# Part of the probabilities-times-values product in three fp32r passes, x loaded twice, and layer norm tails by token tile

## What is computed

```
def _layernorm(x): return (x - mean(x)) / sqrt(var(x) + 1e-5)
# 1: cross-attention, 32 query heads of 128, 4 key/value heads, 4096 + 256 keys
q = latents @ Wq;  k = concat(context, latents) @ Wk;  v = concat(context, latents) @ Wv
attn = softmax(q k^T / sqrt(128));  out = (attn @ v) @ Wo
# 2: linear attention, 32 heads, scores times a causal decay
qkv = silu(h @ qkv_w.T);  scores = q k^T * decay (zero above the diagonal);  attn = scores @ v
normed = norm_w * attn * rsqrt(mean(attn * attn) + EPS)
out = (sigmoid(h @ gate_w.T) * normed) @ out_w.T
# 3: a mixture of 4 low-rank experts of rank 16, the best two weighted by a softmax
x = x + xattn(_layernorm(x), ctx);  x = x + attn(_layernorm(x));  x = x + ffn(_layernorm(x))
```

## Time and profile before

| | us |
|---|---|
| median of three runs | 2026.29 (2024.20 to 2031.31) |
| the profiled execution | 2030.37 |
| its span | 2028.5 |
| TensorE busy in the span | 1987.3 (98%) |
| VectorE, ScalarE, GpSimd busy | 1245.9, 947.0, 776.0 |

### The profile page before, as it was taken

How to read it: one execution, slowest core, us unless ns; L and a number is a source line. 1 busy time by engine, 2 the same in 40 slices (tenths; PEclk the granted TensorE clock), 3 DMA queues, 4 the chain that set the end, 5 groups by cost and what they waited for, 6 DMA issues and landing times. The chain is left out here.

```text
span 2028.5 us, 27101 instructions
## 1 busy us (share of the span) xinstructions
PE 1987.3 (98%) x9797; PEld 1534.1 (76%) x9797; DVE 1245.9 (61%) x1298; ACT 947.0 (47%) x1000; POOL 776.0 (38%) x345
## 2 busy tenths in 40 slices
PE   9999999999999999999999999998999999999998
PEld 7878888876666666566666666655889999999886
DVE  4312221267877767877677877887756666666555
ACT  3112110155665555665565665654634544445442
POOL 2444320026776666766566766762000000000200
PEclk9999999999999999999999999999999999999998
DMA  8788873420032110321112210015735554444461
GB/s 305 297 310 328 323 280 145 174 93 35 13 109 94 65 48 15 112 92 60 43 47 94 78 60 1 6 57 177 278 136 186 186 184 179 176 176 169 157 233 73
DMA packets 72224, 283.85 MB, mean 140 GB/s; under 512 B 6400, under 2 KB 24320, under 8 KB 56512
## 3 DMA queue, kind: packets, MB, share of 16 engines
q1 hardware_dynamic: 72128, 282.65, 38.1%
HBM read 212.89 MB, written 69.73 MB: 139 GB/s over the span
## 5 line engine op out<-in xcount | busy, mean ns | idle before, releaser
L696 POOL TENSOR_TENSOR xa_sums<-xa_sums,stage 128x1024 f32<-128x1024 f32 x150 | 358.4, 2389 | 117.8 <-ACT stage L646 113.5
L883 PE MATMUL xa_o_ps<-stage,xa_v 128*128 128x512 f32 x768 | 362.3, 595 | 5.4 <-ACT stage L646 5.4
L750 DVE TENSOR_TENSOR xa_peak<-xa_s_ps,xa_peak 128x1024 f32<-128x1024 f32 x224 | 274.1, 1223 | 107.0 <-PE xa_s_ps L114 107.0
L112 PE MATMUL xa_s_ps<-xa_qT_hi,split 128*128 128x512 f32 x544 | 306.9, 564 | 6.6 <-issue 3.9
L628 ACT ACTIVATE xa_rows<-xa_s_ps 128x1024 f32<-128x1024 f32 x208 | 213.4, 1026 | 123.5 <-DVE xa_peak L750 107.4
L771 DVE TENSOR_TENSOR xa_rows<-xa_rows,xa_r_ps 128x1024 f32<-128x1024 f32 x208 | 248.4, 1195 | 0.0
L883 PEld LDWEIGHTS xa_o_ps<-stage,xa_v 128*128 128x128 f32 x768 | 144.2, 190 | 124.3 <-issue 106.2
L114 PE MATMUL xa_s_ps<-xa_qT_hi,split 128*128 128x512 f32 x544 | 215.6, 396 | 0.0
L696 POOL TENSOR_TENSOR xa_sums<-xa_sums,xa_probs 128x1024 f32<-128x1024 f32 x75 | 179.2, 2389 | 91.3 <-ACT xa_probs L646 89.8
L113 PE MATMUL xa_s_ps<-xa_qT_lo,split 128*128 128x512 f32 x544 | 213.5, 392 | 0.0
L646 ACT ACTIVATE stage<-xa_rows 128x1024 f32<-128x1024 f32 x144 | 152.4, 1058 | 100.0 <-DVE xa_rows L771 97.5
(11 more groups left out here) (301 smaller groups left out, 4672.2 us busy)
## 6 DMA issues: line engine op xcount, KB each, us to landing
pair_raw<-in_w_qk SPq DMA_DIRECT2D x15, 2048.0 KB, 7.7
pair_raw<-in_w_gv SPq DMA_DIRECT2D x15, 2048.0 KB, 7.6
kv_w_raw<-in_wq SPq DMA_DIRECT2D x16, 1024.0 KB, 7.9
wq_hi_scratch<-x_hT_hi SPq DMA_DIRECT2D x16, 1024.0 KB, 4.3
wq_lo_scratch<-x_hT_lo SPq DMA_DIRECT2D x16, 1024.0 KB, 5.0
full<-in_wo SPq DMA_DIRECT2D x16, 1024.0 KB, 5.2
pair_raw<-in_w_out SPq DMA_DIRECT2D x16, 1024.0 KB, 5.0
xa_w_hi<-wq_hi_scratch SPq DMA_DIRECT2D x15, 1024.0 KB, 4.8
```

What stands on the lines that cost most here:

```text
L112: pe.matmul(out, w_hi, m_hi, start=first, stop=False)
L696: pool.tensor_tensor(sums[:, :, :], sums[:, :, :], probs[j % KEEP], ALU.add).then_inc(added, 1)
L750: dve.tensor_tensor(peak[:, :, :], s_ps[:, 2 * b:2 * b + 2, :], peak[:, :, :], ALU.max).then_inc(peak_done, 1)
L883: last = pe.matmul(o_ps[:, :], v[:, at], probs[j % KEEP][:, t, :], start=j == 0 and t == 0, stop=j == J - 1 and t == 1)
```

## The change

Five of the 17 double tiles of a slot (SPLIT_STEPS, j = 2, 5, 8, 11, 14) multiply their probabilities by their values in `three_pass`. For that ScalarE makes the exponential of such a tile a second time with an fp32r output (`probs_hi`), and GpSimd subtracts it from the fp32 probabilities (`pool_low`), in every slot. The values of these tiles are split once for each of the four key/value heads, in the slots with u = 0: ScalarE rounds them (`act_values`), VectorE subtracts in place (`dve_values`). Values are loaded in more pieces. To make room, x is kept only while the keys and values are made, and is loaded again at the first step of the Wo product.

`LayerNorm` transposes, copies and subtracts by token tile, in two pieces of 128x512 for each, where there were four pieces over both. In `project_out` the last two steps are given in the order of LAST_PARTS, VectorE finishes the rows of token tile 0 before it begins with tile 1, and the idle matmuls are 1 and 13 instead of 8 and 10. In linear attention the second key tile takes only the 128 columns at and after the diagonal, in scores and in values, and the memsets of the zeros are gone.

```diff
+SPLIT_STEPS = (2, 5, 8, 11, 14)
+LOW_BY_VECTOR = ()
...
 class LayerNorm:
-            last = pe.transpose(self.turned[:, k, t * P:(t + 1) * P], self.h[:, t, k * P:(k + 1) * P], self.ident[:, :])
-            if t == QT - 1 and k % 2:
+            last = pe.transpose(self.turned[:, t, k, :], self.h[:, t, k * P:(k + 1) * P], self.ident[:, :])
+            if k % HALF == HALF - 1:
...
+    def act_hi(self, act, t):
+        for b in range(2):
+            k, tok = self.piece(t, b)
+            act.wait_ge(self.turned_ready, 2 * t + b + 1)
+            act.activation(self.hT_hi[:, k, tok], self.turned[:, t, k, :], ACT.Copy).then_inc(self.hi_ready, 1)
...
 def cross_attention(...):
         def act_exp(act, n, j, first=False, last=False):
...
             act.activation(probs[j % KEEP], rows[j], ACT.Exp, scale=SCALE).then_inc(exp_done, 1)
+            if j in SPLIT_STEPS:
+                act.activation(probs_hi[:, :, :], rows[j], ACT.Exp, scale=SCALE).then_inc(probs_hi_ready, 1)
+
+        def act_values(act, g, j):
...
+            act.activation(v_hi[:, split_columns(j)], f32(v_lo[:, split_columns(j)]), ACT.Copy).then_inc(v_hi_ready, 1)
...
+        def pool_low(pool, n, j):
+            pool.wait_ge(exp_done, J * n + j + 1)
+            pool.wait_ge(probs_hi_ready, SPLIT * n + SPLIT_STEPS.index(j) + 1)
+            pool.tensor_tensor(probs_lo[:, :, :], probs[j % KEEP], f32(probs_hi[:, :, :]), ALU.subtract).then_inc(low_by_pool, 1)
...
             for j in range(1, J):
+                if j in (LOW_BY_POOL if has_next else SPLIT_STEPS):
+                    pool_low(pool, n, j)
                 if has_next:
                     pool_add(pool, n, j, not has_prev)
...
+        def dve_values(dve, g, j):
+            at = split_columns(j)
+            dve.wait_ge(v_hi_ready, SPLIT * g + SPLIT_STEPS.index(j) + 1)
+            dve.tensor_tensor(v_lo[:, at], f32(v_lo[:, at]), f32(v_hi[:, at]), ALU.subtract).then_inc(v_lo_ready, 1)
...
         def pe_values(...):
+            if j in SPLIT_STEPS:
+                if values is not None:
+                    pe.wait_ge(v_lo_ready, SPLIT * values + SPLIT_STEPS.index(j) + 1)
...
+                elif not last_slot:
+                    pe.wait_ge(low_by_pool, len(LOW_BY_POOL) * n + LOW_BY_POOL.index(j) + 1)
...
+                for t in range(2):
...
+                    last = three_pass(pe, o_ps[:, :], v_hi[:, at], v_lo[:, at], probs_hi[:, t, :], probs_lo[:, t, :],
+                                      False, False)
+                last.then_inc(pv_done, 1)
+                return
...
+LAST_PARTS = ((0, 0, 0), (0, 0, 1), (0, 1, 0), (1, 0, 0), (1, 0, 1), (0, 1, 1), (1, 1, 0), (1, 1, 1))
...
 def project_out(...):
                     ln.dve_stats(dve, t, half)
-                    if t > 0 and half == 0:
-                        ln.dve_rows(dve, t - 1)
                 ln.dve_variance(dve, t)
-            ln.dve_rows(dve, QT - 1)
-            ln.dve_lo(dve)
+                ln.dve_rows(dve, t)
+            for t in range(QT):
+                ln.dve_lo(dve, t)
...
-            for t, count in zip(range(QT), (8, 10)):
+            for t, count in zip(range(QT), (1, 13)):
...
 def linear_attention(...):
-                    last = three_pass(pe, a_ps[:, h, jt, :], qk_hi[:, h, 1, key], qk_lo[:, h, 1, key],
-                                      qk_hi[:, h, 0, :], qk_lo[:, h, 0, :], True, True)
+                    at = slice(jt * P, TOK)
+                    last = three_pass(pe, a_ps[:, h, jt, at], qk_hi[:, h, 1, key], qk_lo[:, h, 1, key],
+                                      qk_hi[:, h, 0, at], qk_lo[:, h, 0, at], True, True)
...
         def load_first_pair(sp, i):
+            if i == 0:
+                sp.dma_start(x_sb[:, :, :], x).then_inc(x_in, 16)
             weights.load_half(sp, i // 2, i % 2)
```

More of the change, by code:

```diff
@@ L34 @@
 KT = HIDDEN // P
+HALF = KT // 2
 TOK = 256
@@ L471 @@
 LEAD = 2
+SPLIT_STEPS = (2, 5, 8, 11, 14)
+LOW_BY_VECTOR = ()
+LOW_BY_POOL = tuple(j for j in SPLIT_STEPS if j not in LOW_BY_VECTOR)
+SPLIT = len(SPLIT_STEPS)
 KEEP = 3
@@ L482, in starts_piece, with plain_columns, split_columns, value_runs @@
     return j == 0 or j in ENDS
+def plain_columns(j0, j1):
+    back = sum(s < j0 for s in SPLIT_STEPS)
+    return slice(2 * P * (j0 - back), 2 * P * (j1 - back))
+def split_columns(j):
+    i = SPLIT_STEPS.index(j)
+    return slice(2 * P * i, 2 * P * (i + 1))
+def value_runs(i):
+    runs, start = [], ENDS[i - 1] if i else 0
+    for j in range(start, ENDS[i]):
+        if j in SPLIT_STEPS:
+            if start < j:
+                runs.append((start, j))
+            runs.append((j, j + 1))
+            start = j + 1
+    if start < ENDS[i]:
+        runs.append((start, ENDS[i]))
+    return runs
 def cross_attention(nc, wq_drams, k_drams, v_dram, hT_hi, hT_lo, ident, ones, oT_dram, shared, proj, last_pair):
@@ L872, in pe_spread, with pe_values @@
             last.then_inc(spread, 1)
-        def pe_values(pe, n, j, values, first):
+        def pe_values(pe, n, j, values, first, last_slot):
             if j == 0 and not first:
@@ L911, in pe_slot @@
             for j in range(J):
-                pe_values(pe, n, j, values, not has_prev)
+                pe_values(pe, n, j, values, not has_prev, not has_next)
                 if has_next and j + LEAD < J:
@@ L1136, in _ @@
                 step(pe, 2 * i + 1, 1)
-            step(pe, STEPS - 2, 0)
-            pe.wait_ge(proj.lo_ready, SPLITS * STEPS)
-            for t in range(QT):
-                for b in range(2):
-                    for h in range(HP):
-                        last = part(pe, 1, h, t, b, False, h == HP - 1)
+            pe.wait_ge(proj.lo_ready, SPLITS * (STEPS - 1))
+            for par, t, b in LAST_PARTS:
+                if (par, t, b) == (1, 0, 0):
+                    pe.wait_ge(proj.lo_ready, SPLITS * STEPS)
+                for h in range(HP):
+                    last = part(pe, par, h, t, b, False, par == 1 and h == HP - 1)
+                if par == 1:
                     last.then_inc(y_ready, 1)
             pe.wait_ge(x_ready, 1)
-            for t, count in zip(range(QT), (8, 10)):
+            for t, count in zip(range(QT), (1, 13)):
                 keep_clock(pe, y_ps[:, 0, 0, :], proj.s_hi[1][:, 0, 0:P], proj.w_hi[1][:, 0, 0:BANK], count)
```

111 lines of the change are left out of this document (72 added, 39 removed).

## The result

| | before | after |
|---|---|---|
| median, runs side by side | 2025.24 us, 4 runs (2023.94 to 2031.31) | 2053.43 us, 4 runs (2051.62 to 2055.06) |
| profiled execution, its span | 2030.37, 2028.5 | 2053.17, 2051.4 |
| mean granted clock | 0.991 | 0.990 |

The ratio is 1.0133, with a 95% interval from 1.0114 to 1.0152: the change makes the kernel slower by 28 us. The forecast was 2071, so the sign and the wait for GpSimd came as forecast, and 17 us of the cost did not.

A forecast was written before the change was run, and what follows sets the result against it. The prediction took GpSimd's added subtractions, in a chain from slot to slot, to bound the kernel instead of TensorE. Its terms 27 + 16 + 6 - 2 - 3 + 1 = +45 took 2026.3 to about 2071 us, range 2036 to 2098.

The forecast's parts named there:

- closed chain: From tile 14's values to the same place one slot later: 61.9 us, 62.5 with VectorE's fold, against 60.70 before; +27.
- Part one: From tile 14's values to the next slot's subtraction of tile 2, including two exponentials: 19.5 us.
- Part two: GpSimd without a pause from the subtraction of tile 2 to that of tile 14: 42.4 us.
- The fold of the maxima: VectorE's L753 waits for GpSimd's running operation, then takes its own 0.69 us; adds 0.6 us to each slot's period.
- Values split in slots with u = 0: VectorE's value subtractions wait for GpSimd and hold scores back: 4 us in each of 4 slots, +16, bounds 7 and 28.
- Rival 2: Slots cost less, as fold and value subtractions slip between GpSimd's operations and the last slot has room: +15, about 2041; chance 0.17.
- The last slot: GpSimd's 33.6 us and VectorE's seven additions can't run side by side, 42.6 in a row: +6, bounds 0 and 10.
- Linear attention: 192 matmuls of 128 columns for 256, limited by weight loads, each 0.013 us shorter: -2.
- rival 3: Narrow fp32r matmuls in linear attention run in four passes like plain fp32: +18 instead of -2, 2091; chance 0.15.
- Tails and x: Two tails of 1.7 us less each, -3, bounds 0 and -6; loading x again, +1, bounds 0 and 3.
- Rival 4: The clock falls in TensorE's new waits before tiles 11 and 14 of each slot: 15 us more, 2086; chance 0.13.
- Rival 1: GpSimd keeps up with its subtractions, so TensorE's 26 us are gained: -30, 1996; chance 0.10.

The follow-up runs named there:

- experiment 3: The changed kernel with ScalarE's second exponential cut to 8 columns of each half; 2043.86 us in one run, steady period 60.89 us.
- experiment 6: The changed kernel with four split tiles (2, 6, 10, 14) instead of five; 2021.52 us, 0.9979 of the kernel before, period 59.64 us.
- experiment 9: The changed kernel with four split tiles at (2, 5, 8, 11) and no GpSimd subtractions in the last slot; 2039.84 us in one run, period 61.84 us.
- experiment 5: The changed kernel with GpSimd's sums of tiles 15 and 16 and its sum over the halves cut to 8 columns; 2055.93 us in one run, period 61.70.
- experiment 1: The changed kernel with GpSimd's subtraction of the probabilities cut to 8 columns of each half; 2006.26 us, 0.9909 of the kernel before.
- experiment 11: The changed kernel with tile 8's subtraction given to VectorE and no GpSimd subtractions in the last slot; 2036.24 us, 1.0050 of the kernel before.
- experiment 10: The changed kernel with five split tiles at (2, 5, 8, 12, 15) and no GpSimd subtractions in the last slot; 2037.11 us in one run, period 61.35.
- experiment 7: The changed kernel with no GpSimd subtractions in the last slot, where split tiles use whole probabilities in plain fp32 plus one fp32r pass; 2044.52 us.

## Why the prediction was right, and where its sizes were off

**The closed chain: right, and right in size.** Part one, from the values of tile 14 (673.61) to the next slot's subtraction of tile 2 (one period behind 631.44): 631.44 + 61.72 - 673.61 = 19.5, forecast 19.5. Part two: 631.44 to 673.56 (671.17 + 2.39) is 42.1, forecast 42.4. The forecast's sum was 61.9, and 61.7 was measured. Experiments 3, 6 and 9 move members of the chain and the period follows; experiment 5 takes work away beside it and the period stays; experiment 1 takes it out and TensorE's own 58.9 appears.

**The fold of the maxima: a term that had no place in the chain, 0.6 us in a slot.** The forecast put L753 into the chain. In the trace of after its median is longer still:

```profile
L825 DVE TENSOR_TENSOR xa_peak<-xa_peak x16: 693/2708/2892, 424.1 to 1352.2; 128x512 f32<-128x512 f32 x16
```

But it starts at 671.40, behind GpSimd's subtraction of tile 14 (671.17), waits for that one's end, and delays only the sum behind it: 2.86 at 673.52 instead of 2.4. That sum is no part of the chain. (This is read from the trace; no experiment was made on the fold alone.) I had asked whether the fold excludes GpSimd, but not which of GpSimd's operations it meets. Without it the forecast's term is 15 x 1.2 = 18 instead of 27, and 15 x 1.02 = 15 was measured.

**Values split in slots with u = 0: 0.8 us each, forecast 4.** That is 3 instead of 16 in sum, the term of the forecast that was furthest off. The forecast let each subtraction wait 1.2 us in the mean for GpSimd's running operation, 6 us in a slot beside 2.1 us of their own, and passed 4 of the 8 us on to the slot. Their durations after, and the same line in experiment 3:

```profile
L855 DVE TENSOR_TENSOR xa_v_lo<-xa_v_lo,xa_v_hi x20: 416/644/1917, 442.6 to 1224.9; 128x256 fp32r<-128x256 f32 x20
```

```profile
L859 DVE TENSOR_TENSOR xa_v_lo<-xa_v_lo,xa_v_hi x20: 417/1330/2551, 443.8 to 1223.5; 128x256 fp32r<-128x256 f32 x20
```

In the change the median wait is 0.2 us, and VectorE's busy time rises by 2.7 us in such a slot. In experiment 3 GpSimd has the same operations at slightly other times; there the median wait is 0.9, and VectorE's busy time rises by 6.9 us (47.0 to 53.9). TensorE's waits in that slot of experiment 3:

```profile
PE xa_s_ps L113 <- ACT xa_rows L683: 1.4, 2, 1.0
PE xa_o_ps L113 <- POOL xa_probs_lo L768: 1.3, 2, 0.9
```

It waits for scores as well as for GpSimd, and the slot is 2.6 us longer than a steady one. Experiments 1 and 11 are alike (VectorE 6.3 and 6.5 us more, the slot 2.5 and 4.3 longer); experiments 6, 9 and 10 are like the change (3.2, 2.0 and 3.9 more, the slot 0.6, 0.6 and 1.0 longer). So the mechanism exists, with up to 4.8 of the forecast's 6 us of waiting, and what failed for the change is the size of the wait: its subtractions mostly missed GpSimd's operations. That it is their place in time that decides is read from the traces; no run moved these subtractions alone. Rival 2 said of fold and values that they would slip between GpSimd's operations: for these two terms it was the better text, and the result, 2053, lies between its 2041 and the forecast's 2071. Its last slot (0) was further off than the forecast's.

**The last slot: +12, forecast +6.** The forecast added durations: 33.6 of GpSimd and 9.0 of VectorE, 42.6 in a row against 37.6 before, which is +5 and not the +6 that it wrote. In the trace GpSimd's operations take up to 3.35 and VectorE's additions up to 3.40, since each stands for the other:

```profile
1385.00 3.11 POOL L766 TENSOR_TENSOR xa_probs_lo<-xa_probs,xa_probs_hi 128x1024 fp32r<-128x1024 f32 x1 [1.91 <-ACT xa_probs_hi L702]
1388.07 2.38 POOL L795 TENSOR_TENSOR xa_sums<-xa_sums,stage 128x1024 f32<-128x1024 f32 x1
1390.42 2.26 POOL L779 TENSOR_TENSOR head_out<-xa_o_raw,xa_inverse 128x512 f32<-128x512 f32 x1
1393.32 3.28 POOL L766 TENSOR_TENSOR xa_probs_lo<-xa_probs,xa_probs_hi 128x1024 fp32r<-128x1024 f32 x1 [0.64 <-ACT xa_probs_hi L702]
```

GpSimd also idles (1.91, 0.64) for exponentials, which wait for VectorE, which waits for GpSimd. The engine that fills the slot is VectorE: with the same 30 operations it is busy for 43.8 of 49.6 us, and for 35.6 of 37.6 before. The forecast left out all of VectorE's work there but the additions. Experiment 7 gives 10 of the 12 us back, and experiment 1 all of them. The clock fell too, 0.83 against 0.96; whether that cost the slot time by itself no experiment separated.

**Linear attention: right.** From its first matmul to the last group of la_o before and after, 2.0 us less, forecast 2. Two groups of 256 and of 128 columns in order of time:

```profile
1929.67 0.28 PE L114 MATMUL la_o_ps<-split 128*128 128x256 f32 x1
1929.79 0.28 PE L115 MATMUL la_o_ps<-split 128*128 128x256 f32 x1
1929.90 0.22 PE L113 MATMUL la_o_ps<-split 128*128 128x128 f32 x1
1929.96 0.28 PE L114 MATMUL la_o_ps<-split 128*128 128x128 f32 x1
1930.07 0.27 PE L115 MATMUL la_o_ps<-split 128*128 128x128 f32 x1
```

A narrow one is 0.06 to 0.11 from the next, no four passes: rival 3 has fallen. The starts of single ones vary; over 192 the sum says 0.010 each, the size of a weight load's limit.

**Tails and x.** The Wo tail, from the last matmul before it (1507.69) to the end of the low parts (1515.77), takes 8.1 us instead of 10.0; but the stage as a whole, sums to linear attention, is 0.3 longer, since TensorE waits 1.1 us more in it. The other stage is 2.3 shorter. Together -2.0; forecast -3 and +1.

**Rival 4, the clock.** In the steady slots the waits are 1.5 and 0.4 us and the clock stays at 1.00: refuted there. But in its profiled execution before had two slots at 0.97 (64.4 and 64.7 us long), and the same slots take 63.5 after, at 1.00. That is about 4 us for the changed kernel, and the forecast had no term for it. The pauses ahead of them differ: 1.86 us and 2.07 before, 1.44 and 1.47 after. They differ between executions of the same code as well. Experiment 7 is the change up to the last slot, and its pauses are 1.70, with the clock at 1.00, and 1.77, with the clock at 0.97. After, and experiment 7:

```profile
1000.66 0.49 PE L113 MATMUL xa_s_ps<-xa_qT_hi,split 128*128 128x512 f32 x1 [1.47 <-issue]
```

```profile
1001.93 0.53 PE L113 MATMUL xa_s_ps<-xa_qT_hi,split 128*128 128x512 f32 x1 [1.77 <-issue]
1002.26 0.63 PE L114 MATMUL xa_s_ps<-xa_qT_lo,split 128*128 128x512 f32 x1
```

So the 4 us belong to the executions that were profiled, and nothing shows that the change won them.

**Rival 1** was refuted by the period. It said that it would need subtractions under 2.1 us; by the forecast's own chain 2.1 takes the period only to 60.5, and the 59.1 that gives 26 us needs 1.8. Experiments 1 and 6 show what it would have taken.

In sum, for the profiled executions: steady slots 15, u = 0 slots 3, last slot 12, linear attention -2, tails and x -2, the clock -4, together 22 of 22.9 us of span. Against the medians it is 28, and without the clock's -4 the terms are 26: the profiled execution of before lay 5 us above its median, that of after did not.

## What to carry to other kernels

Lay the chain from the last consumer of one round to the first producer of the next and count only the work between those two ends: neither busy shares nor the load of a slot (52.8 of 61.7 us here) tell that an engine is the bound, and the same four tiles at another place cost 2.2 us more per slot. For an operation that stands whenever it meets one of another engine's, give a range and not a mean: a slot with the same five subtractions of values is 0.8 us longer than a steady one in the change and 2.6 in experiment 3. And look at the last round by itself, where other engines than in the steady ones have time to spare: 10 us lay there in one slot of sixteen.

## What was not expected of the hardware

- VectorE and GpSimd exclude each other both ways and cost both: a VectorE operation of 0.69 us lasted 2.7, and the GpSimd operation behind it 2.86 or 3.27 instead of 2.4. Handing an operation of 2.39 us to VectorE won 1.3. How often two such operations meet shifts with small changes elsewhere.
- Two profiled executions with nearly the same mean clock (0.991 before, 0.990 after) had their falls at different places: before behind two pauses of 1.86 and 2.07 us in the middle of slots, after behind two waits of 5 us in the last slot.
